# One pass over all three shares' expert steps, with the gates' matrix built inside them

## What is computed

```python
logits = xf @ Wr + br
topk_logits, topk_idx = jax.lax.top_k(logits, TOP_K)          # TOP_K = 2
gates = jax.nn.softmax(topk_logits, axis=1)
combine = jnp.zeros((T, E)).at[jnp.arange(T)[:, None], topk_idx].add(gates)
for e in range(E):
    h = jax.nn.relu(xf @ W1[e] + b1[e])
    y = h @ W2[e] + b2[e]
    out = out + combine[:, e:e + 1] * y
```

## Time and profile before

| what | us |
|---|---|
| median of three runs | 900.72 |
| the profiled execution's own time | 901.74 |
| its span, first to last instruction | 899.9 |
| first `y_copy` starts | 524.2 |
| last `y_copy` starts | 793.3 |
| PE, DVE, ACT, POOL busy | 520.3, 571.1, 330.5, 595.1 |

### The profile page before, as it was taken

The page is one execution under the profiler, slowest core; times in us unless marked ns, Lnnn a source line. Parts: engine busy times, 40 slices in busy tenths (PEclk is TensorE's granted clock), DMA queues, the critical chain, the costliest instruction groups (busy, mean ns, idle before and its releaser), DMA issues.

```text
span 899.9 us, 9083 instructions
## 1 busy us (share of the span) xinstructions
PE 520.3 (58%) x2514; PEld 348.0 (39%) x2520; DVE 571.1 (63%) x1180; ACT 330.5 (37%) x622; POOL 595.1 (66%) x393
## 2 busy tenths in 40 slices
PE   4653344675576666667357578868767678720050
PEld 4643111221222222234234367747656567610050
DVE  1697899999999999978256623323223223284258
ACT  2169756466556555433113123323222223200020
POOL 5894699999999999913644645635655365557700
PEclk9857578798887797877568788988998799975575
DMA  7999900000000000000350257776876678211102
GB/s 245 383 160 119 48 1 0 0 0 0 0 1 0 0 0 0 0 0 23 86 142 15 69 162 223 196 206 193 230 212 183 185 213 233 59 41 27 26 1 92
DMA packets 106605, 84.96 MB, mean 94 GB/s; under 512 B 30464, under 2 KB 90240, under 8 KB 106560
## 3 DMA queue, kind: packets, MB, share of 16 engines
q1 hardware_dynamic: 79312, 54.76, 28.2%
q10 hardware_dynamic: 19184, 21.40, 7.7%
q0 software_dynamic: 8064, 8.27, 3.6%
HBM read 57.22 MB, written 33.49 MB: 101 GB/s over the span
## 4 chain that ended last, share of the span: by engine, by line
PE 27%; DVE 26%; issue 16%; POOL 13%; ACT 8%; another core or an unknown queue 8%; SPq 1%; DMA 1%; POOLq 0%; DVEq 0%; ACTq 0%
PE ps L907 11%; POOL x_w L576 7%; POOL w_ring L569 6%; PE ps L894 5%; DVE hh_ring L1422 4%; DVE x_w L1616 2%; DVE hh_ring L1633 2%; PE ps L672 2%; ACT ps L1067 2%; DVE x_w L1606 2%; DVE w_ring L1416 2%; ACT ps L1073 2%; PE ps L736 2%; DVE us_lg L1633 2%
## 5 line engine op out<-in xcount | busy, mean ns | idle before, releaser
L736 PE MATMUL ps<-x_w,ident 128*128 128x512 f32 x252 | 151.6, 760 | 102.5 <-POOL x_w L576 102.5
L626 POOL DMA_INDIRECT sorted_rows<-xp,slot_i x126 | 122.0, 968 | 124.2 <-DVE x_w L1616 42.9
L647 POOL DMA_INDIRECT xt<-expert_out,slot_i x126 | 119.9, 952 | 91.0 <-DVE x_w L1616 52.2
L569 POOL TENSOR_TENSOR w_ring<-xt,bc 128x2016 f32<-128x2016 f32 x32 | 144.7, 4522 | 13.5 <-DVE hh_ring L1422 7.3
L1422 DVE TENSOR_TENSOR_SCAN hh_ring<-ps,w_ring 128x1024 f32<-128x1024 f32 x64 | 145.6, 2275 | 0.1
L576 POOL TENSOR_TENSOR x_w<-hh_ring,bc 128x2016 f32<-128x2016 f32 (+1 forms) x32 | 142.4, 4454 | 0.9 <-PE ps L736 0.9
L736 PEld LDWEIGHTS ps<-x_w,ident 128*128 128x128 f32 x252 | 59.2, 245 | 197.7 <-POOL x_w L576 125.8
L1616 DVE COPY x_w<-ps 128x256 f32<-128x256 f32 x80 | 33.9, 424 | 128.4 <-PE ps L907 63.6
L1073 ACT ACTIVATE ps<-dt_t,a_exp 128x1024 f32<-128x1024 f32 x64 | 71.5, 1117 | 64.2 <-DVE hh_ring L1422 64.2
L1067 ACT ACTIVATE ps<-dt_t,a_exp 128x1024 f32<-128x1024 f32 x64 | 71.5, 1118 | 52.1 <-DVE w_ring L1401 52.1
L1164 ACT ACTIVATE x_w<-ps 128x256 f32<-128x256 f32 x80 | 30.6, 383 | 156.4 <-PE ps L883 95.6
(11 more groups left out here) (209 smaller groups left out, 915.8 us busy)
## 6 DMA issues: line engine op xcount, KB each, us to landing
dt_t<-packed SPq DMA_DIRECT2D x140, 96.5 KB
x_w<-packed SPq DMA_DIRECT2D x112, 96.5 KB
x_w<-sorted_rows ACTq DMA_DIRECT2D x40, 256.0 KB
expert_out<-x_w ACTq DMA_DIRECT2D x80, 128.0 KB
sorted_rows<-pad_rows SPq DMA_DIRECT2D x2, 3584.0 KB, 24.1
bc<-packed SPq DMA_DIRECT2D x68, 96.5 KB
packed<-in_L_ffn_W SPq DMA_DIRECT2D x3, 2048.0 KB, 38.7
x_w<-in_x SPq DMA_DIRECT2D x7, 448.0 KB, 9.7
```

What stands on the lines that cost most here:

```text
L569: pool.tensor_tensor(w_buf(k, 2), up3[:, bass.ds(c * DC, DC), 1:S].unsqueeze(1).broadcast_to([P, 2, DC, L]), vec_of(k, 2), ALU.mult).then_ ...
L626: pool.indirect_dma_start(out=sorted_rows[h], out_offset=bass.IndirectOffsetOnAxis(ap=slot_i[:, c, l:l + 1], axis=0), in_=xn[:, l, :], in_ ...
L647: pool.indirect_dma_start(out=y[:, l, :], out_offset=None, in_=expert_out[h], in_offset=bass.IndirectOffsetOnAxis(ap=slot_i[:, c, l:l + 1] ...
L736: ins = pe.matmul(ps[:, i, :], ident[:, :], src[:, i * BANK:(i + 1) * BANK], start=(k < 0), stop=(k == (N - 2 if last else N - 1)), skip_g ...
```

## The change

On PE, ACT and DVE the loops over shares are replaced by one loop over all 80 steps. The wait for a share's sent rows moves to the load of its first unit, which now is issued four units ahead, among the steps of the share before. DVE's 126 operations that build `combine` are spread over steps 0 to 62, two per step behind the `y_copy`, and the eight sums over steps 8, 16, ..., 64. PE's, ACT's and DVE's work behind the last step is otherwise as it was, and so are POOL's and SP's programs.

```diff
@@ tensor @@
-            for h in range(len(SHARES)):
-                a, z = STEP0[h], STEP0[h + 1]
-                rows_T(a)
-                rows_T(a + 1)
-                hidden(a)
-                for i in range(a, z):
-                    if i + 2 < z:
-                        rows_T(i + 2)
-                    if i + 1 < z:
-                        hidden(i + 1)
-                    outputs(i)
+            rows_T(0)
+            rows_T(1)
+            hidden(0)
+            for i in range(STEP0[-1]):
+                if i + 2 < STEP0[-1]:
+                    rows_T(i + 2)
+                if i + 1 < STEP0[-1]:
+                    hidden(i + 1)
+                outputs(i)
@@ scalar @@
+            def rows_of_unit(u):
+
+                if u in UNIT0:
+                    h = UNIT0.index(u)
+                    act.wait_ge(s_disp[h], 16 * 2 * (SHARES[h][1] - SHARES[h][0]))
+                load_rows(act, u)
+
             def next_rows(i):
 
-                h = share_at(STEP0, i)
-                d = i - STEP0[h] + 1
+                d = i + 1
                 u = d // (UNIT // 2) - 1 + RING
-                if d % (UNIT // 2) == 0 and u < UNITS[h]:
-                    load_rows(act, UNIT0[h] + u)
+                if d % (UNIT // 2) == 0 and u < UNIT0[-1]:
+                    rows_of_unit(u)
...
@@ vector @@
-            for h in range(len(SHARES)):
-                a, z = STEP0[h], STEP0[h + 1]
-                relu_B(a)
-                for i in range(a, z):
-                    if i + 1 < z:
-                        relu_B(i + 1)
-                    y_copy(i)
-
             gates = (top[:, 5, :], gate2[:, :])
-            for k in range(2):
-                dve.memset(comb[k][:, L, :], 0.0).then_inc(s_dve, 1)
-                ch.at = ch.at + 1
-                for l in range(L):
-                    last = dve.tensor_scalar(comb[k][:, l, :], iota_e[:, :], top[:, 2 + k, l:l + 1], gates[k][:, l:l + 1],
-                                             ALU.is_equal, ALU.mult)
-                    last.then_inc(s_dve, 1)
-                ch.at = ch.at + L
-            dve.wait_ge(s_dve, ch.at)
-            for q in range(CQ):
+
+            def gates_at(l):
+
+                for k in range(2):
+                    dve.tensor_scalar(comb[k][:, l, :], iota_e[:, :], top[:, 2 + k, l:l + 1], gates[k][:, l:l + 1],
+                                      ALU.is_equal, ALU.mult).then_inc(s_dve, 1)
+                ch.at = ch.at + 2
+
+            def both_gates(q):
+
                 span = slice(8 * q, 8 * (q + 1))
+                dve.wait_ge(s_dve, ch.at)
                 dve.tensor_tensor(comb[0][:, span, :], comb[0][:, span, :], comb[1][:, span, :], ALU.add
                                   ).then_inc(s_comb, 1)
+
+            for k in range(2):
+                ch.link(dve.memset(comb[k][:, L, :], 0.0))
+            relu_B(0)
+            for i in range(STEP0[-1]):
+                if i + 1 < STEP0[-1]:
+                    relu_B(i + 1)
+                y_copy(i)
+                if i > 0 and i % 8 == 0 and i // 8 <= CQ:
+                    both_gates(i // 8 - 1)
+                if i < L:
+                    gates_at(i)
```

33 lines of the change are left out of this document (15 added, 18 removed).

## The result

The changed kernel takes **874.15 us** (median of four runs, 873.01 to 875.2), the kernel before in the same sitting 899.73 us (four runs, 898.38 to 900.98). The ratio is 0.9716, with a 95% interval of 0.9693 to 0.9739. The forecast was 844.5, its range ended at 866; the gain is 25.6 us where 55 were forecast. The profiled execution took 874.86 us, its span is 873.0.

A forecast was written before the change was run, and what follows sets the result against it. The prediction saw a sequence of stages, no engine busy over 66%, steps paced by POOL's four DMAs and one copy. Span 899.9 - 17.7 (edges) - 38.5 (end) = 843.7, time 844.5 us; range 837 to 866.

The forecast's parts named there:

- The edges: Between shares: the two gaps of 12.82 and 12.31 us become ordinary steps of 3.24 us, saving 17.7 us (16.7 to 18.7).
- The gates' matrix in the steps at nothing: Expert steps: DVE's added operations fit where it waits anyway, costing nothing; 188 us if nothing hid them.
- the hold: Steps and sort: signals between engines can be held while POOL issues indirect DMAs, coming through when POOL pauses.
- The end, -38.5: Behind the last copy: sums leave the path, bias term and parts go beside POOL's fetches; 38.5 us less.
- DVE alone on the path: Behind the last fetch's start: 47 of the last 106.6 us, said to hang on DVE only.
- the bias chain is held: Behind the last step: PE's signal held until POOL pauses, all 36 operations stay behind; 861 to 879 us, chance 0.12.
- The end's picture: Behind the last copy: DVE takes parts as they land; only four operations and a store follow the last fetch.
- DVE late at the end: Rival, last stretch: DVE slowed beside POOL's 46 DMAs, last four parts still open at 860.4; 854.4 us, chance 0.17.
- Edges stay: Rival, between shares: POOL late or ACT held at its moved wait, so 17.7 us don't come; 862 us, chance 0.07.
- Gates slow the steps: Rival, steps: DVE's added signals queue, each operation costs on the path; ends above 900.7 us, chance 0.05.
- the fetches themselves do not move: Behind the last copy: POOL's fetches begin 3.0 us later, 56.6 us to the last, 0.95 for it.

## Why the prediction was wrong

**The edges: right mechanism, size off in one profile.** The gaps went by 18.7 us as worked out. The pace inside the shares isn't fixed to 3.24 us, though. The same loop took 256.0, 250.6, 249.0, 253.7, 253.6, 253.4 and 253.6 us in seven profiles of the four sittings with a hold, 252.8 on average, which is 16.3 less than 269.1; forecast were 17.7, with 16.7 as the lower bound. It is the scatter of the held steps, which I had taken for a constant. That the pace is set by POOL's four DMAs and one copy wasn't shown: where nothing is held, the same DMAs lie in steps of 2.37 us.

**The gates' matrix in the steps at nothing: right** (256.4 against 256.0 us, 267.6 against 269.1). By the Trainium skill ("SBUF — State Buffer", Who interferes with whom) a `tensor_scalar` in a two-port mode can delay POOL; whether these ran in one the trace doesn't tell. No run shows a delay by them: the DMAs at 601.17 and 602.43 have 0.95 us each and 1.26 us between them, with L1626 and L1607 running in between, and the steps take 2.37 us with the operations as without. That it was the hold that hid them isn't so: where nothing is held they cost nothing either.

**The end, -38.5: this step failed.** The prediction wrote "the bias term can start at 793.8: 793.8 + (875.0 - 860.4) = 808.4 at the latest, while POOL fetches". That took the chain's duration from a stretch in which POOL was silent (860 to 875) and put it into one in which POOL issues 46 DMAs. It measured 68.5 us from the last copy, not 14.6. In the same vein the text has "DVE alone on the path" behind the last fetch, although the bias term there goes through PE and ACT. This was the rival "the bias chain is held", given 0.12, with its case quoted in the text, and its place and mechanism came out: signals of PE late, the last pieces behind POOL's last fetch, 36 operations behind them. Its argument against, that the chain has 3 us ahead of the first fetch and needs 11 to 15, was no argument: three or four of eight pieces get through in that time. Its price, 861 to 879, holds the result, 874. The chances were the mistake. In the old trace ACT and PE hand each other work beside a long burst of POOL's (21 DMAs, the first at 417.88 and the last at 443.51) in the sort, and there it was held; the steps, where hand-overs did get through, had bursts of four.

**The end's picture is right once the chain is out of the burst.** With the bias term in the steps the kernel takes 850.9, with it ahead of the fetches 858.5. The first is 6.4 us above the forecast. 5.0 us of the difference is the last store, forecast at 2.05 us by a row in which the fetches were over, measured at 7.0 right behind them, and 1.8 the slower fetches (58.35 us from first to last in this kernel, forecast 56.6).

**The other rivals.** DVE late at the end by its own work: no, its 20 linked operations ran at 0.72 us beside the fetches. Edges stay: no. Gates slow the steps: no.

**What stays open.** What the hold is, why it is there in four sittings and absent in two, and why 0.08 us more between DMAs, or 0.02 us and a pause, shorten it from about 68 to 36 to 38 us behind the last copy. Why it falls on PE's hand-overs and not on those to PE, and whether it is PE's signal or its work that is late. That a long burst of POOL's, the hold and the held chain belong together is shown by three kernels (POOL waiting, fetches left out, chain in the steps); the cause underneath is not.

## What to carry to other kernels

When work moves beside another engine's long burst of DMAs, take its duration from a stretch with such a burst in it, not from a quiet one; where hand-overs were held, a chain through PE paid for every hand-over from PE, and a queue that worked alone (20 operations of DVE, 0.72 us each) paid nothing. When a wait has no named releaser, compare the end of the row that it waits for with its own start, engine by engine: that tells whose signals are late. Here it paid to put the chain ahead of the burst (POOL waiting 10.5 us for it won 12 to 16) or far from it, into the steps (20 us against the changed kernel of the same sitting), and to let only work that waits for the DMAs themselves stand beside them. And before giving up "useless" columns on PE, look at the granted clock: two thirds less columns in the second layer made the 80 steps together 17 us slower.

## What was unexpected in the hardware

- Late were the waits for PE, by up to 40.0 us, and never PE's waits for ACT or DVE (0.05 us in the bias term, at most 0.15 us in the steps).
- The kernel before took 896 to 901 us in four sittings and 775 to 777 us in two, the changed one 871 to 874 and 757. In the changed kernel's profile of the latter no hand-over is late, steps take 2.37 us, and POOL's indirect DMAs are as long (0.95 us) and as close (1.26 us) as ever.
- Where the last store follows right behind the burst of indirect DMAs, the span ends 5.6 to 7.4 us behind DVE's last operation (849.7 for bytes moved by 844), also where nothing else is held: 749.46 to 756.5 in the changed kernel's profile of the last sitting. Where the burst is long over it is 2.0 us.
- POOL's fetches get longer beside DVE's operations on the parts. Two rows that group them over a stretch (busy us, mean ns of one, idle before): in the last sitting's profile of the changed kernel, 694 to 710 us, with parts beside them, and in the first one, 784 to 838 us, without:

```profile
L647 POOL DMA_INDIRECT xt<-expert_out,slot_i x12 | 13.2, 1103 | 3.7 <-issue 3.7
```
```profile
L647 POOL DMA_INDIRECT xt<-expert_out,slot_i x44 | 41.8, 951 | 13.4 <-issue 13.4
```

  1.10 us with them (0.95 without, or with the bias term's additions, which read one operand from PSUM). The 46 fetches then take 58.4 to 59.2 us, not the 56.6 of the earlier trace rows, so the forecast's "the fetches themselves do not move" was 2 to 3 us short. The Trainium skill ("SBUF — State Buffer", Who interferes with whom) says that a VectorE operation with two SBUF inputs contends with a GpSimd instruction that reads SBUF; these operations have two, and the trace agrees, with 0.15 us a fetch.
- PE's granted clock fell from 0.97 to 0.67 of full speed when its second layer had 64 columns instead of 192, with the same number of matmuls, and was back at 0.97 with 192.
